# Decay sums of a gated delta-rule layer: four transposes and a masked scan on VectorE instead of a product with a triangle of ones

## The reference

```python
g = -jnp.exp(A_log) * jax.nn.softplus(a + dt_bias)      # log decay, one number per token and value head

def step(S, xs):
    qt, kt, vt, gt, bt = xs
    S = S * jnp.exp(gt)[..., None, None]                 # the state decays at each token
    kv = jnp.einsum('bhk,bhkv->bhv', kt, S)
    delta = (vt - kv) * bt[..., None]
    S = S + jnp.einsum('bhk,bhv->bhkv', kt, delta)
    o = jnp.einsum('bhk,bhkv->bhv', qt * scale, S)
    return (S, o)
```

## Time and profile before

| what | value |
|---|---|
| median of 3 runs | 4777.71 us (4777.23 to 4779.94) |
| the profiled execution | 4782.79 us, of which the span of the instructions is 4781.0 us |
| TensorE (PE) busy | 4586.8 us, 96% of the span |
| VectorE (DVE) busy | 2680.7 us, 56% |
| ScalarE (ACT) busy | 2348.9 us, 49% |
| GpSimd (POOL) busy | 1387.1 us, 29% |

### The profile page before, as it was taken

How to read it: one execution, slowest core, us unless ns; L and a number is a source line. 1 busy time by engine, 2 the same in 40 slices (tenths; PEclk the granted TensorE clock), 3 DMA queues, 4 the chain that set the end, 5 groups by cost and what they waited for, 6 DMA issues and landing times.

```text
span 4781.0 us, 81715 instructions
## 1 busy us (share of the span) xinstructions
PE 4586.8 (96%) x30056; PEld 3134.5 (66%) x30056; DVE 2680.7 (56%) x6818; ACT 2348.9 (49%) x5714; POOL 1387.1 (29%) x1542
## 2 busy tenths in 40 slices
PE   7999999997899999999999999999999999999998
PEld 3444444443777777777777777777777777777775
DVE  3222222212666666666666666666676666667664
ACT  1000111101566656666666666666666666666664
POOL 1000000000233333333333333333343333434333
PEclk9999999998999999999999999999999999999998
DMA  3000000002000000000000001100000000010000
GB/s 132 19 27 25 22 24 27 18 9 94 6 10 10 10 12 10 10 10 10 10 10 17 10 28 45 34 23 23 29 26 23 23 23 23 23 37 23 23 19 30
DMA packets 72605, 118.46 MB, mean 25 GB/s; under 512 B 12432, under 2 KB 29456, under 8 KB 72208
## 3 DMA queue, kind: packets, MB, share of 16 engines
q1 hardware_dynamic: 72208, 113.22, 7.1%
HBM read 79.09 MB, written 34.11 MB: 24 GB/s over the span
## 4 chain that ended last, share of the span: by engine, by line
PE 63%; DVE 10%; issue 1%; ACT 1%; POOL 0%; SPq 0%; DMA 0%; DVEq 0%; POOLq 0%; ACTq 0%
PE bank L806 18%; PE bank L810 10%; PE bank L1169 9%; PE bank L1448 7%; DVE vraw L836 3%; PE bank L1086 2%; PE bank L1342 2%; PE bank L1356 2%; PE bank L1382 2%; PE bank L1294 2%; PE bank L1317 2%; PE bank L1070 1%; PE bank L945 1%; PE bank L1071 1%; PE bank L812 1%
## 5 line engine op out<-in xcount | busy, mean ns | idle before, releaser
L806 PE MATMUL bank<-xtile,wt 128*128 128x259 f32 x4096 | 1083.0, 396 | 79.2 <-DVE vraw L836 50.9
L806 PEld LDWEIGHTS bank<-xtile,wt 128*128 128x128 f32 x4096 | 725.5, 191 | 214.3 <-DVE vraw L836 81.1
L1228 ACT ACTIVATE xyinv<-bank 128x512 f16<-128x512 f32 x768 | 457.4, 596 | 365.0 <-PE bank L1169 362.5
L1206 DVE TENSOR_TENSOR wlev<-bank,mask 128x256 f16<-128x256 f32 x768 | 320.9, 420 | 469.6 <-PE bank L1169 467.0
L1448 PE MATMUL bank<-wot,xnt 128*128 128x512 f32 x1024 | 532.8, 611 | 0.9 <-ACT xnt L1441 0.8
L810 PE MATMUL bank<-wt,xtile 128*128 128x512 f32 x1024 | 523.4, 617 | 0.0
L836 DVE SCALAR_TENSOR_TENSOR vraw<-bank,taps,vraw 128x256 f32<-128x256 f32 x768 | 370.2, 482 | 126.7 <-ACT vraw L829 105.5
L370 DVE TENSOR_TENSOR hid<-bank,gate 128x512 f32<-128x512 f32 x88 | 60.9, 692 | 521.1 <-PE bank L352 521.1
L1146 POOL TENSOR_TENSOR kend<-ktok,bend 128x256 f32<-128x256 f32 x256 | 158.6, 640 | 636.3 <-issue 635.8
L1169 PEld LDWEIGHTS bank<-xyinv,lth 128*128 128x128 f16 x3584 | 220.7, 98 | 167.3 <-issue 108.5
L347 PE MATMUL bank<-h2t,wg_sb 128*128 128x512 f32 x704 | 318.4, 595 | 0.0
(11 more groups left out here) (179 smaller groups left out, 9327.0 us busy)
## 6 DMA issues: line engine op xcount, KB each, us to landing
xtile<-xt_scratch SPq DMA_DIRECT2D x32, 518.0 KB, 4.1
xn<-x SPq DMA_DIRECT2D x32, 256.0 KB, 5.3
xt_scratch<-xt SPq DMA_DIRECT2D x8, 1024.0 KB, 5.8
g_scratch<-sel SPq DMA_DIRECT2D x32, 256.0 KB, 2.0
wt<-w_qkvz SPq DMA_DIRECT2D x4, 2048.0 KB, 13.2
part_scratch<-prow SPq DMA_DIRECT2D x32, 256.0 KB, 2.1
prow<-part_scratch SPq DMA_DIRECT2D x32, 256.0 KB, 2.7
grow<-g_scratch SPq DMA_DIRECT2D x32, 256.0 KB, 3.5
```

The lines of the kernel that those rows point to most:

```text
L806: j = pe.matmul(b_p[:, 0:WIN], wt[:, k, c:c + P], xtile[:, par, k, :], **st)
L1206: dve.tensor_tensor(wlev[:, lv - 1].rearrange("p h (b t s) -> p h b t s", t=2, s=z)[:, :, :, 0, :], b_inv[p][:, 0:HEADS * P // 2].rearrang ...
L1228: act.activation(dst, b_inv[p][:].rearrange("p (a h b s) -> p a h b s", a=2, h=HEADS, s=z), ACT.Copy).then_inc(s[f"xy_sb{p}"], 1)
```

## The change

The decay sums are now made in two steps. TensorE writes, for each of the 4 heads, a transpose of the column g[:, h] repeated 128 times: every row of the result holds g of the 128 tokens. VectorE then runs a scan along the 512 columns of bank 3, state = (state + g) * mask, with a new mask `M_PAST` that is 1 where r < c and 0 elsewhere: the state stays 0 up to column r and then adds up g, and it starts anew at each head. ScalarE takes the exp in place, from `gam` and no longer from PSUM. GpSimd's `pool_decay` and tile `gm` are gone. Bank 3 is free once the scan has read it (semaphore `sum_sb`), no longer when the exp has.

```diff
-N_MASK = M_EVEN + (LEVELS - 1) // 2
+M_PAST = M_EVEN + (LEVELS - 1) // 2
+N_MASK = M_PAST + HEADS
...
+    m[:, M_PAST:] = (r[:, None] < r[None, :])[:, None, :]
...
         def pe_gate(pe, c):
             tile, cc = divmod(c, CPT)
             if c:
-                pe.wait_ge(s["gam_sb"], NB * c)
+                pe.wait_ge(s["sum_sb"], NB * c)
...
-        def pool_decay(pool, n):
-
-            c, m, tile, cc = where(n)
-            if n:
-                pool.wait_ge(s["gam_ps"], n)
-            pool.wait_ge(s["gt_sb"], (tile + 1) * N_GATE)
-            pool.tensor_tensor(gm[:], le.unsqueeze(1).broadcast_to([P, HEADS, P]),
-                               gdec[:, tile % 2, cc, unit_heads(m)].unsqueeze(2).broadcast_to([P, HEADS, P]), ALU.mult).then_inc(s["gm_sb"], 1)
...
         def pe_decay(pe, n):
 
+            c, m, tile, cc = where(n)
             pe.wait_ge(s["kq_sb"], n + 1)
-            pe.wait_ge(s["gm_sb"], n + 1)
-            pe.matmul(b_a[:], gt, gm[:].rearrange("p h c -> p (h c)"), start=True, stop=True).then_inc(s["gam_ps"], 1)
+            for h in range(HEADS):
+                g = gdec[:, tile % 2, cc, m * HEADS + h:m * HEADS + h + 1]
+                i = pe.transpose(b_a[:, h * P:(h + 1) * P], g.broadcast_to([P, P]), ident)
+            i.then_inc(s["gr_ps"], 1)
+
+        def dve_decay(dve, n):
+
+            dve.wait_ge(s["gr_ps"], n + 1)
+            if n:
+                dve.wait_ge(s["pt_sb"], n)
+                dve.wait_ge(s["lt_sb"], n)
+            dve.tensor_tensor_scan(gam[:].rearrange("p h c -> p (h c)"), b_a[:], mask[:, M_PAST:, :].rearrange("p h c -> p (h c)"), 0.0, ALU.add, ALU.mult).then_inc(s["sum_sb"], 1)
 
         def act_decay(act, n):
-            act.wait_ge(s["gam_ps"], n + 1)
-            if n:
-                act.wait_ge(s["pt_sb"], n)
-                act.wait_ge(s["lt_sb"], n)
-            act.activation(gam[:], quad(b_a), ACT.Exp).then_inc(s["gam_sb"], 1)
+            act.wait_ge(s["sum_sb"], n + 1)
+            act.activation(gam[:], gam[:], ACT.Exp).then_inc(s["gam_sb"], 1)
...
-                ("pe", "decay"): [("dve", "scores", n), ("pool", "decay", n)],
-                ("act", "decay"): [("pe", "decay", n), ("dve", "attend", n - 1)],
+                ("pe", "decay"): [("dve", "scores", n)],
+                ("dve", "decay"): [("pe", "decay", n), ("dve", "attend", n - 1)],
+                ("act", "decay"): [("dve", "decay", n)],
```

32 lines of the change are left out of this document (14 added, 18 removed), and 2 rows, old and new, of the table TAKES.

## The result

The changed kernel takes 4862.76 us (median of 4 runs, 4860.0 to 4864.7), the kernel before in the same comparison 4777.48 us: ratio 1.0177, 95% interval 1.0159 to 1.0195. The forecast was 4737 us.

The account below looks back on a forecast made before the run. TensorE, 98% busy in the steady stretch, was taken as the bound. Transposes -52, new waits +10, first unit and mask +1 made -41 from 4782.8: 4742 us; the median lies 5.1 lower, so 4737, range 4720 to 4765.

Parts of the forecast that it names:

- The transposes: TensorE's decay step: four transposes take 0.43 us for the matmul's 0.86, saving 52 us over 120 units (all 128: 55).
- The scan: New VectorE pass over 128x512 from PSUM, once a unit: 1.2 us each, 154 us in all.
- the 5 us that were forecast: VectorE's `ltm` and `pt` lose 48 us to stalls beside GpSimd; with `gm` gone, some 5 us come back.
- unit 50: New order laid over the trace there: 0.9 us of slack, so new waits end before TensorE asks.
- Rival 2: Taps and scans between key or query blocks make VectorE the bound: at a 2.4 us scan, 4796 us; chance 0.06.
- rival 3: Transposes give TensorE nothing, through slow column loads or the lower clock: 4789 us, or 4778; chance 0.05.
- rival 1: Gain half eaten by tap waits in the dense stretch, 0.9 us lost per tile: 4755 us; chance 0.13.
- signs named: Confirming signs: transposes 0.43 us, scan 1.1 to 1.3, TensorE 97 to 98% busy, tap waits 45 to 60 us, slightly fewer stalls.
- All three that were to show it wrong: TensorE's tap or scan waits up over 30 us, scan over 1.3 us, or transposes over 0.5 us.
- Where the scan lies: VectorE's dense stretch, where key and query blocks are projected; closes by taking 0.3 us a tile, 10 us, of new waits.
- Nothing on the path: ScalarE's exp (3 us) and table loads (18 us) hidden, GpSimd loses work; 1 us for first unit and longer mask.
- other orders of the planned lists: Leftover case of the planner ordering the lists otherwise, with effect either way; chance 0.04, no size given.

Follow-up runs that it names:

- e3: Changed kernel with the scan cut to 128 of its 512 columns and the exp using head 0's sums for all four heads: 4861.45 us (1.0170).
- e8: Changed kernel with one planner cost altered, VectorE's gate operations at 4.8 in place of 3.2: 4863.93 us (1.0180).
- e1: Changed kernel with 24 useless full-precision transposes put on TensorE ahead of each tile's first gate product wait: 4826.33 us (1.0097).
- e2: Changed kernel with each tile's first gate product moved later on TensorE, behind the next tile product and the query transposes: 4886.06 us (1.0223).
- e4: Changed kernel with each tile's learn product moved up on TensorE, ahead of two output products and the tile product: 4848.65 us (1.0144).
- e7: Changed kernel with VectorE's gate series behind three taps, and TensorE's gate product behind the next tile product and query transposes: 4840.64 us (1.0133).
- e10: Changed kernel with an output product and the error's sum moved behind the last ba product, and the learn product moved earlier: 4862.29 us (1.0175).
- e12: Changed kernel, three tiles of four: two output products moved behind the learn product, the error's sum behind the second keys product: 4812.99 us (1.0070).
- e13: e12 with the learn product also ahead of the tile product, and moves of its own in every fourth tile: 4813.76 us (1.0073).
- e15: e13 with scan and exp moved behind the last query taps, and VectorE's first gate operations moved ahead of a waiting step: 4886.47 us (1.0223).
- e18: e17 with one output product of every fourth tile moved behind the second keys product: 4800.02 us (1.0046).
- e6: Kernel before, with two output products per tile moved ahead of the last query product; no scan, no new transposes: 4809.1 us (1.0066).
- e11: Kernel before, with two output products moved from behind the keys product to ahead of the ba product: 4832.48 us (1.0114).
- e17: e13 with every fourth tile redone: output products stay ahead of the first keys product, VectorE's first gate operations go earlier: 4800.65 us (1.0047).
- e14: Kernel before, with two output products moved from behind the learn product to ahead of it; no scan: 4826.63 us (1.0098).
- e5: Changed kernel's operations in the old kernel's order, transposes and scan put in by hand: 4912.44 us (1.0282).

## Why the prediction was wrong

**Right.** The transposes: 0.43 us a unit saved; the work column has -62 us, against the 52 to 55 that these are worth; the rest was not traced further. The scan: 1.218 us for 1.2. The Trainium skill ("DVE: opcode table, instruction layouts, handler registers and perf-mode slots", section "Datapath and trigger behaviour") gave, with its half throughput, an estimated 1.15 us; this trace agrees within 6%. `ltm` became faster (401 to 348 ns), `pt` slower (384 to 429): their stalls over 342 ns sum to 43 us for 48, the 5 us that were forecast, but only as a sum. The place that the prediction worked through, unit 50, opened no wait: for the scan TensorE waits 0.4 us once in the whole run, and taps 29 us for 45. Rival 2 (VectorE becomes the bound) and rival 3 (transposes give nothing) did not come true, rival 1 (taps) neither; e3 bears this out for the scan's load. In rival 2 the sum has a slip: with the stall gone the rows give 18.7 + 2s and not 18.5 + 2s, so the excess would begin at s = 1.2 and not at 1.3; nothing hung on it. Of the signs named, only one spoke against the forecast: TensorE is 96.1% busy (3170.8 of 3300 us), not 97 to 98%. All three that were to show it wrong (waits for taps or scan, the scan's length, the transposes' length) stayed silent, since all three looked where the prediction looked.

**The step that failed** is "Where the scan lies", with the sentence that closes it and "Nothing on the path": the search for new waits looked at the banks and the scores near the scan, and took all else in the lists as unmoved. It took the taps for what TensorE waits for on VectorE, because they were 44.8 of 67 idle us. But a chain that has 0.3 us to spare shows in a table of waits as next to nothing, here as 0.2 us. The lists of all engines were made anew, and in them two output products and the error's sum stand ahead of the learn and keys products. (Which new cost or dependency moved them was not tried apart; e8 changed one cost and moved next to nothing here.) The learn cover of 3.6 us against a chain of 5.9 us leaves some 2.4 us a tile, in every fourth 2.7 or 4.8: the term of +78 us was missing altogether. Most of it could have been read blind: the order of the changed kernel was there, and the durations are in the trace of before. There the learn chain is 5.3 us long, so that the new cover of 3.6 leaves an estimated 1.7 us a tile, some 50 us over 29 tiles. The rest is the series, which became 0.5 us longer.

**A second term was missing:** the price of a gap is not its length. Behind each gap of 2.4 to 4.8 us the clock is at its lower level, and that doubled the loss (+70 us). e1 shows it apart from the gap (half clock 14 us for 140). The prediction named the clock only in rival 3, for the transposes.

**The chance of 0.04 for "other orders of the planned lists"** was where the result lay. Twelve of the kernels here differ from the change as it came in nothing but order (e2, e4, e7 to e10, e12, e13, e15 to e18), and they span 4800 to 4886 us, more than the whole change was forecast to bring. e6 and e11 say the same of the old kernel: two moved output products cost 32 and 54 us.

**What stays open.** e17 has all the gain in its work column (-57) and is still behind: in the profiled executions by 14 us, idle +53 and half clock +19; in the medians by 24 us, as the profiled execution of before is 5 us above its median and that of e17 3 us below. The waits name where: taps +7, gate 17.7, `xyinv` of the chain +4, `tsq` 9.6 in three places, keys 6.6, learn +6. Whether lists exist in which all of these are covered, so that the forecast's 4737 us is reached, was not found out; no version here beats the kernel before. Whether the 7 us of work beyond 55 are real is open, and so is where all of e6's 32 us and e11's 54 us go. That the gate waits and the clock behind them are the larger part of the loss rests on e1 (the clock), e12 and e17 (cover put back: 50 and 62 of 85 us) and e14 (the learn cover cut in the old kernel: 49 us).

## What to carry to other kernels

Where a planner or a scheduler orders the work, ask of every chain that leaves the bounding engine and comes back how much of that engine's work lies between, before and after the change, and compare it with the chain's length; the chains that wait for nothing today are the ones to list, since a table of waits shows hardly anything of their slack. Look also at what runs on GpSimd beside a chain of small VectorE operations, since a shift by a microsecond changes the chain's length. Gaps of 2.4 us and more on TensorE cost about twice their length here (78 us of waits, 70 us by the clock), though not every gap of 2 us does. And when an engine at 98% is relieved by 2%, expect other chains to be within that 2%. Here it was not the work taken away that uncovered the chain, but two output products of 0.86 us that the planner listed elsewhere.

## What the runs showed of the hardware

- **The half clock follows a gap of TensorE's, but not every gap, and transposes in the gap prevent it.** Waits of 0.5 us for taps by the dozen do not lower it (before, e6); the gaps of 2.4 us and more did each time in the changed kernel (29 of 29), and those of 0.7 to 1.1 us sometimes (e12, e14). The length alone does not decide: none followed the seven tap waits of 1.6 us in e6 and in e11, e5 has 29 waits of 2.0 us for `wlev` but 11 stretches at half clock in all, and in e2 two of the 28 gaps of over 2 us (3.75 us, for taps, at 2422.8 and 3911.0) left the granted clock at 1.00. What else decides, no run here shows. The Trainium skill ("TensorE: Matmul & The Clock Gate", section "Part 4: PE-mode transpose") says that a transpose does not count as activity in the way a matmul does. e1 speaks against it for full-precision ones, at least for fillings of 2.8 us between matmuls: its gaps are filled with nothing but transposes, and the clock stays at 1.00 in all tiles but the three where 2.0 us of gap were left.
- **Some small VectorE operations end only with the GpSimd instruction beside them.** In e4 L991 took 0.97 us for 0.25 and ended 0.03 us after a GpSimd multiplication of 1.04 us (L898), and so did L993, L994 and L995 behind the next ones; in the changed kernel it was the first operation alone (L989, 0.88 us). The reciprocals between them kept their 0.25 us (L992 in e4), and the 1.67 us GpSimd instruction on 128x8 (L892) held up none. The Trainium skill ("SBUF — State Buffer", section "SBUF: two separate sides") has the two share a port pair that one of them holds for a whole instruction, VectorE only with two SBUF inputs or in a fast mode; that agrees with L993 and L994, which have two such inputs. L991 and L995 have one, and no row shows in which mode they ran.
- **A scan costs 1.78 times a plain pass** of the same shape (1218 ns at L1090 and 683 ns at L1072 for 128x512 from PSUM with a mask), and it hardly varies: 1210 to 1225 ns in all 128.
